# One core, four transformer sub-layers: key weights loaded in two parts, three turns put in another order, and one PSUM bank for each weighted value product

## What is computed

```python
x = x + tanh(g_xattn[0]) * causal_attention(q=layernorm(x), k=ctx, v=ctx)     # 16 heads of 32
x = x + tanh(g_ffn[0]) * ffn_ternary_silu(layernorm(x), w_gate_up, w_proj)    # hidden 2048, weights quantised per 64
x = x + tanh(g_xattn[1]) * cross_attention(layernorm(x), ctx, q_w, k_img_w, v_img_w, o_w, ...)   # 256 keys, rms norm of q and k
x = x + tanh(g_ffn[1]) * bitlinear_ffn(layernorm(x), w_gv, w_out)             # ternary weights, 8-bit activations
```

## Time and profile before

| | |
|---|---|
| median of 3 runs | 1153.73 us (1153.06 to 1154.17) |
| the profiled execution | 1155.84 us, its span (first to last instruction) 1154.0 us |
| TensorE busy | 1112.5 us, 96% of the span |
| VectorE busy | 833.0 us, 72% |
| ScalarE busy | 566.9 us, 49% |
| TensorE's mean granted clock | 0.988 of full |

### The profile page before, as it was taken

One profiled execution on the slowest core, in us unless ns is written; L12 is line 12 of the kernel. 1 busy time (PEld: TensorE's weight loads), 2 busy tenths in 40 slices (PEclk: granted clock), 3 DMA queues, 4 the chain that ended last, 5 costly groups with the idle time before them and its releaser, 6 DMA issues.

```text
span 1154.0 us, 25637 instructions
## 1 busy us (share of the span) xinstructions
PE 1112.5 (96%) x10450; PEld 672.7 (58%) x10450; DVE 833.0 (72%) x1440; ACT 566.9 (49%) x918; POOL 74.2 (6%) x180
## 2 busy tenths in 40 slices
PE   8899999998899999999999999899999999999998
PEld 3455555555677777777777654445454545454543
DVE  5688888777566657566565667687877878777785
ACT  3676666764333333333333442445463737372754
POOL 0000000000000000000001011010101010101010
PEclk9899999999899999999999999999999999999999
DMA  9555555433111010120110201101010100000001
GB/s 371 170 191 175 183 184 174 142 109 111 47 56 41 25 56 19 37 74 19 37 56 19 82 3 37 37 2 56 1 57 1 33 24 17 22 11 11 10 10 37
DMA packets 29124, 79.24 MB, mean 69 GB/s; under 512 B 3025, under 2 KB 3281, under 8 KB 28625
## 3 DMA queue, kind: packets, MB, share of 16 engines
q1 hardware_dynamic: 29008, 77.61, 20.4%
HBM read 65.02 MB, written 12.58 MB: 67 GB/s over the span
## 4 chain that ended last, share of the span: by engine, by line
PE 90%; DVE 5%; ACT 2%; issue 2%; DMA 1%; POOL 0%; ACTq 0%; SPq 0%; DVEq 0%; POOLq 0%
PE bank L537 10%; PE bank L579 10%; PE bank L580 10%; PE bank L662 10%; PE bank L682 9%; PE bank L785 8%; PE bank L773 5%; PE bank L423 5%; PE bank L815 5%; PE bank L735 3%; PE bank L754 3%; PE bank L472 2%; PE bank L493 2%; PE bank L505 2%; PE bank L448 2%
## 5 line engine op out<-in xcount | busy, mean ns | idle before, releaser
L579 PE MATMUL bank<-ARENA,W 128*128 128x256 f16 x1024 | 228.7, 274 | 1.6 <-issue 1.6
L580 PE MATMUL bank<-ARENA,W 128*128 128x256 f16 x1024 | 228.7, 274 | 0.0
L989 ACT ACTIVATE ARENA<-bank 128x512 f32<-128x512 f32 (+3 forms) x143 | 92.9, 689 | 86.3 <-PE bank L423 31.4
L537 PE MATMUL bank<-ARENA 128*128 128x512 f32 x256 | 120.3, 614 | 2.0 <-DMA ARENA<-in_wkv 2.0
L662 PE MATMUL bank<-W,ARENA 128*128 128x512 bf16 x512 | 121.0, 379 | 0.7 <-DVE ARENA L1399 0.7
L785 PE MATMUL bank<-W,ARENA 128*128 128x512 bf16 x512 | 119.6, 383 | 0.7 <-DVE W L1697 0.3
L682 PE MATMUL bank<-ARENA 128*128 128x512 f32 x256 | 116.8, 599 | 0.0
L579 PEld LDWEIGHTS bank<-ARENA,W 128*128 128x128 bf16 x1024 | 100.5, 98 | 20.8 <-issue 2.3
L580 PEld LDWEIGHTS bank<-ARENA,W 128*128 128x128 bf16 x1024 | 100.5, 98 | 18.2
L1557 DVE SCALAR_TENSOR_TENSOR ARENA<-bank,ARENA 128x512 f32<-128x512 f32 x64 | 48.0, 750 | 83.7 <-PE bank L580 78.2
L989 ACT ACTIVATE ARENA<-ARENA 128x512 f16<-128x512 f32 x64 | 40.3, 630 | 130.9 <-DVE ARENA L1557 128.1
(11 more groups left out here) (179 smaller groups left out, 1787.6 us busy)
## 6 DMA issues: line engine op xcount, KB each, us to landing
W<-in_w SPq DMA_DIRECT2D x48, 512.0 KB, 4.1
ARENA<-in_w SPq DMA_DIRECT2D x24, 512.0 KB, 3.6
kv_store<-ARENA SPq DMA_DIRECT2D x32, 256.0 KB, 4.2
W<-kv_store SPq DMA_DIRECT2D x15, 512.0 KB, 3.9
ARENA<-in_ctxT SPq DMA_DIRECT2D x8, 512.0 KB, 3.8
X<-in_x SPq DMA_DIRECT2D x8, 512.0 KB, 6.2
ARENA<-in_ctx SPq DMA_DIRECT2D x8, 512.0 KB, 5.8
out<-X SPq DMA_DIRECT2D x16, 256.0 KB, 2.1
```

Of the source, the lines that this page charges most:

```text
L537: mm = pe.matmul(bank, bufA["KT"][:, b % 2 * KD + k, t * P:(t + 1) * P], W[:, k, :], start=(k == 0), stop=(k == KD - 1 and what == 1))
L579: pe.matmul(bank[:, i * S:(i + 1) * S], W0[:, at:at + P], xt_half(b, 0)[:, k, :], start=(k == 0), stop=False)
L580: mm = pe.matmul(bank[:, i * S:(i + 1) * S], W0[:, at:at + P], xt_half(b, 1)[:, k, :], start=False, stop=(k == KD - 1))
L989: return act.activation(to, src, ACT.Copy)
```

## The change

Five things are edited. (1) The 1 MB of key weights is loaded as two halves of 512 KB with the bias row (`vec`) between them, and `a_project` waits for the second half (`ld_wk2`) ahead of its third input block. (2) In turns 1 and 8 (`late`) VectorE does the second block of scores, `a_max_parts` and `a_max_rows` ahead of `a_ternary(b, 0)`. (3) In turn 8 the first input of stage B is normalised, transposed (into banks 6 and 7) and split earlier, on all engines; the last value projection `a_project(7, 3)` goes to its former place, into bank 1; the largest weight (`m_largest`) is found ahead of `a_max_rows(b, 1)`, and `a_ternary(7, 2)` comes after the whole chain of `m_scl`. (4) At the start of stage B `a_turn_sums(7)` goes to bank 5 and lies between the two parts of `b_gate_up(0, 1)`, and `b_project(0, 0)` comes after `b_gate_up(0, 2)`. (5) In the first turns of stage C each weighted value has a bank of its own, `c_turn_x(1)` moves behind `b_project(7, 6)`, and in the turn of sequence 1 `c_project_q(2, 1)` comes ahead of the output products, and `c_max_rows(1)` ahead of `c_add_out(0, 1)`. Turns 2 to 7 of stage A, stage B after its first three steps, and stage C from turn 3 on are left as they were.

```diff
--- before.py
+++ after.py
-    ld_cst ld_gc ld_x0 ld_x1 ld_kt0 ld_kt1 ld_rv0 ld_rv1 ld_w00 ld_w01 ld_w02 ld_w1a ld_w1b ld_wk ld_wv ld_sel ld_wqo ld_kb ld_row ld_wn
+    ld_cst ld_gc ld_x0 ld_x1 ld_kt0 ld_kt1 ld_rv0 ld_rv1 ld_w00 ld_w01 ld_w02 ld_w1a ld_w1b ld_wk ld_wk2 ld_wv ld_sel ld_wqo ld_kb ld_row ld_wn
...
-        diag = scrA["t"].bitcast(F32)[:, 0:P]
+        diag = scrA["raw0"][:, 0, 0:P]
...
         def bank_of_kv(b, i):
-            return 5 if (b, i) == (0, 1) else (1, 1, 6, 7)[i]
+            return {(0, 1): 5, (NB - 1, 3): 1}.get((b, i), (1, 1, 6, 7)[i])
...
-        places.last = {4: (s.a_pvr, 2 * NB), 5: (s.a_sumr, 2 * NB), 6: (s.b_xy, 2 * NB - 1), 7: (s.b_xy, 2 * NB),
+        places.last = {4: (s.a_pvr, 2 * NB), 5: (s.a_otr, 3 * NB - 2), 6: (s.b_xy, 2 * NB - 1), 7: (s.b_xy, 2 * NB),
...
-        places.turn(1, ("pq0 xt0", "pq1 tq1 w1 w2 w3", "mt kt0 w0", "kt1 tq0 xt1"))
-        for turn in range(2, NB):
+        places.turn(1, ("pq0 kt0 w0 xt0", "pq1 tq1 w1 xt1", "mt tq0 w2", "kt1 w3"))
+        places.turn(2, ("pq0 po0 w0 xt0", "po1 w1 qt1 w3", "pq1 kt0 tq1 w2", "kt1 mt tq0 qt0 xt1"))
+        for turn in range(3, NB):
             places.turn(turn, ("g0 v1 g3 pq0 v6 v7 ut0.0 y0 xt0", "v0 po1 v3 g4 v5 g7 tq1 w1 w2 w3", "po0 g2 kt0 v4 pq1 w0 qt1 ut1.1 y1",
                                "g1 v2 kt1 g5 g6 mt tq0 ut0.1 qt0 ut1.0 xt1"))
...
-            sp.dma_start(bufA["wkv"][:, 0, :], wkv[:, 0:KD * D]).then_inc(s.ld_wk, 16)
+            sp.dma_start(bufA["wkv"][:, 0, 0:2 * D], wkv[:, 0:2 * D]).then_inc(s.ld_wk, 16)
             sp.dma_start(bufA["tmp"][:, 0, :], vec[:, 0:D]).then_inc(s.ld_kb, 16)
+            sp.dma_start(bufA["wkv"][:, 0, 2 * D:KD * D], wkv[:, 2 * D:KD * D]).then_inc(s.ld_wk2, 16)
...
                 if (b, g) == (NB - 1, 2):
-                    pe.wait_ge(s.b_xl, 2)
+                    pe.wait_ge(s.a_kvr, 4 * NB)
...
+                if (b, g) == (NB - 1, 0):
+                    pe.wait_ge(s.b_xl, 2)
                 for j in range(4):
-                    pe.wait_ge(*ringA[4 + j].freed(f"pr{g}", b + 1))
+                    if (b, g, j) != (NB - 1, 0, 3):
+                        pe.wait_ge(*ringA[4 + j].freed(f"pr{g}", b + 1))
...
             def a_turn_sums(turn, b):
-                pe.wait_ge(*ringA[1].freed("ot2", turn))
+                if b < NB - 1:
+                    pe.wait_ge(*ringA[1].freed("ot2", turn))
                 pe.wait_ge(s.a_sumr, 2 * b + 2)
-                turned(banks[1], [scrA["SS"][:, half, t * P:(t + 1) * P] for half in range(2) for t in range(TB)],
+                turned(banks[1 if b < NB - 1 else 5], [scrA["SS"][:, half, t * P:(t + 1) * P] for half in range(2) for t in range(TB)],
                        keep["identf"]).then_inc(s.a_ot, 1)
...
-                    pe.wait_ge(*ringA[at].freed(f"kv{i}", turn))
+                    pe.wait_ge(*ringA[at].freed("kv0" if (b, i) == (NB - 1, 3) else f"kv{i}", turn))
                 for k in range(KD):
+                    if not what and k == 2:
+                        pe.wait_ge(s.ld_wk2, 16)
...
                         to, sem, value = bank_c(f"bx{t}", f)
                         pe.wait_ge(sem, value)
                     else:
-                        to = banks[1 - t]
-                        pe.wait_ge(*(ringA[0].freed("sc2", NB) if t else ringA[1].freed("kv0", NB)))
+                        to = banks[6 + t]
+                        pe.wait_ge(*((s.a_ex, 16 * (NB - 2) + 14) if t else (s.a_kvr, 4 * NB - 1)))
                     pe.wait_ge(s.b_xn, 2 * f + t + 1)
...
                 if q == 1:
                     pe.wait_ge(s.m_scl, 1)
-                    pe.wait_ge(s.a_otr, 3 * NB - 2)
...
                 a_scores(b, 1)
+                if not front:
+                    b_turn_x(0)
                 if end:
                     a_sum(turn, e, 1)
+                if end and front:
                     a_project(turn, b, 3)
                 a_group_sum(turn, b, 1)
...
                 if front:
                     a_project(turn, f, 0)
                 else:
-                    b_turn_x(0)
+                    a_project(turn, b, 3)
                 a_probs(b, 1)
                 a_scores(b, 2)
...
             for b in range(NB):
                 last = b == NB - 1
                 for p in range(8):
-                    if p or b:
-                        b_gate_up(b, p)
                     if (b, p) == (0, 0):
                         b_gate_up(0, 0, (1,), (1,))
                         a_weigh(NB + 1, NB - 1, 1)
                         a_sum(NB + 1, NB - 1, 1)
+                    elif (b, p) == (0, 1):
+                        b_gate_up(0, 1, (0,))
                         a_turn_sums(NB + 1, NB - 1)
-                    if (b, p) == (0, 1):
+                        b_gate_up(0, 1, (1,))
                         a_turn_out(NB + 1, NB - 1)
+                    else:
+                        b_gate_up(b, p)
+                    if (b, p) == (0, 2):
+                        b_project(0, 0)
...
                     elif not last or p < 6:
-                        if p or b:
+                        if p > 1 or b:
                             b_project(*divmod(8 * b + p - 1, 8))
-            c_turn_x(1)
-
             c_scores(0, 0)
             b_project(NB - 1, 6)
+            c_turn_x(1)
             c_scores(0, 1)
             b_project(NB - 1, 7)
             b_sum_squares(NB - 1)
...
             c_scores(1, 0)
             c_project_q(2, 0)
             c_scores(1, 1)
+            c_project_q(2, 1)
+            c_scores(1, 2)
             c_project_out(0, 0)
-            c_scores(1, 2)
             c_turn_k(2)
+            c_scores(1, 3)
             c_project_out(0, 1)
-            c_scores(1, 3)
-            c_project_q(2, 1)
             c_max_turn(1)
             c_probs(1, 0)
             c_turn_q(2)
...
                 if end:
                     a_weighed(e, 1)
+                    if not front:
+                        b_turn_x(0)
                     a_summed(e, 1)
                 if front:
                     a_signs(f, 0)
-                a_projected(b, 3)
+                    a_projected(b, 3)
...
                 if front:
                     a_projected(f, 0)
                 else:
-                    b_turn_x(0)
+                    a_projected(b, 3)
                 a_probs(b, 1)
...
             c_square_q(2, 0)
+            c_square_q(2, 1)
             c_turn_k(2)
-            c_square_q(2, 1)
             c_probs(1, 0)
             c_turn_q(2)
...
+                    sums = banks[5 if b == NB - 1 else 1].rearrange("p (a t j c) -> p a t j c", a=2, t=TB, c=DH)[:, :, t, :, 0:2]
...
+            def m_largest():
+                v.wait_ge(*own.now())
+                v.tensor_reduce(hs[:, 2:3], keep["wmax"], AX_X, ALU.max).then_inc(*own.up())
+                v.wait_ge(*own.now())
+                v.tensor_scalar(hs[:, 2:3], hs[:, 2:3], 1e-8, None, ALU.max).then_inc(*own.up())
+                v.wait_ge(*own.now())
+                v.tensor_scalar(diag, keep["identf"], hs[:, 2:3], None, ALU.mult).then_inc(s.m_in, 1)
+
             for turn in range(NB + 1):
                 f, b, e, last = turn, turn - 1, turn - 2, turn - 3
                 front, back, end = f < NB, b >= 0, e >= 0
+                late = turn in (1, NB)
                 if back:
                     a_scores(b, 0)
+                    if not front:
+                        v.wait_ge(s.a_xt, 2 * NB)
+                        v.wait_ge(s.b_rstd, 1)
+                        for t in range(TB):
+                            normed(0, t, bufB["xn"]).then_inc(s.b_xn, 1)
                     a_distance(b, 0)
-                    a_ternary(b, 0)
+                    if not late:
+                        a_ternary(b, 0)
                     a_scores(b, 1)
                     a_max_parts(b, 0)
+                    if not front:
+                        b_turn_x(0)
+                    if late:
+                        a_max_rows(b, 0)
                 if front:
                     v.wait_ge((s.ld_x0, s.ld_x1)[f % 2], 16 * (f // 2 + 1))
                     stats(f, s.a_ve)
-                else:
...
-                if back:
+                if back and not late:
                     a_max_rows(b, 0)
...
-                else:
-                    v.wait_ge(s.a_xt, 2 * NB)
-                    v.wait_ge(s.b_rstd, 1)
-                    for t in range(TB):
-                        normed(0, t, bufB["xn"]).then_inc(s.b_xn, 1)
...
                 if end:
                     a_reciprocals(e)
+                if late:
+                    a_ternary(b, 0)
                 if last >= 0:
                     a_add_out(last)
                 if back:
                     a_distance(b, 1)
-                    if not front:
-                        b_turn_x(0)
                     a_ternary(b, 1)
                     a_scores(b, 2)
...
                 if back:
                     a_scores(b, 3)
```

(32 more changed lines are left out.)

8 lines of the change are left out of this document (1 added, 7 removed).

## The result

The changed kernel took 1140.55 us (median of 4 runs, 1139.14 to 1142.06) beside 1153.57 us of the kernel before (4 runs); the ratio is 0.9887, its interval 0.9870 to 0.9904. That is 13.0 us faster, where 17.1 us were forecast. Run again beside other kernels it took 1140.13 us beside 1153.93 us, ratio 0.9873 (0.9854 to 0.9892). The profiled execution took 1139.14 us, with a span of 1137.4 us.

A forecast was written before the change was run, and what follows sets the result against it. TensorE was taken as the bound, losing time to idle waits and half clock in three places. Gains of 2.2 + 11.3 + 3.6 = 17.1 us gave 1136.6 us, within 2.5 us at chance 0.70; 1132 to 1142 us at 0.85.

The forecast's parts named there:

- Part 1: Start of the kernel: key halves bring the first projection some 1.3 us earlier, counted as nothing because a store's landing holds.
- Part 2: Turn 1: VectorE's new order moves a_probs(0, 0) from 33.29 to 31.05 us; 2.2 us gained together with the key halves.
- Part 3: Turn 8 and entry to stage B: 13.8 us of waits and low clock, less new waits, gives 11.3 us.
- Three of the new waits: Turn 8 and stage B entry: 0.55 us for last scores at b_gate_up, 0.6 at a_probs(7, 3), 1.0 at a_weigh(7, 1).
- the 0.4 us at `a_probs(7, 0)`: Turn 8: VectorE's two subtractions between the maxima and their copy make a_probs(7, 0) wait about 0.4 us.
- the two long waits: Turn 8: 2.9 us for the largest weight's chain and 2.6 us at a_scores(7, 2) for b_xl; both were to go.
- Part 4: First turns of stage C: separate banks and new orders remove waits, one of 2.2 us remains at c_turn_x(3); 3.6 us gained.
- More than forecast: Turn 0's stores land earlier (2.4 us) or clock stays up after c_turn_x(3) (1.7 us); both give 1132.5 us; chance 0.12.
- Low clock in turn 8: Rival: four short waits keep TensorE at 1.2 GHz in turn 8, losing 3.3 us, 1140 us; chance 0.12.
- Waits that only move: Rival: turn 8's 9 us reappear in stage B's first b_project, time within 2 us of 1153.7 us; chance 0.03.

The follow-up runs named there:

- whole_keys: The changed kernel with the key weights loaded whole again; 1139.73 us, ratio 0.9883 to the kernel before.
- c_only: The kernel before with only stage C's separate banks and changed orders; 1151.02 us, ratio 0.9974.
- t8_only: The kernel before with only the changes to turn 8 and the entry to stage B; 1143.48 us, ratio 0.9908.
- before_store: The kernel before with the first two stores queued ahead of four loads, nothing else; 1155.20 us, ratio 0.9998.
- t1_only: The kernel before with only the key halves and VectorE's new order in turn 1; 1156.18 us, ratio 1.0015.
- no_t1: The changed kernel with whole keys and VectorE's old order in turn 1; 1140.93 us, ratio 0.9884 to the kernel before.
- early_store_whole: The changed kernel with the first two stores queued ahead of four loads and key weights loaded whole; 1140.18 us, ratio 0.9863 to the kernel before.
- after_again: The changed kernel itself, measured again; 1140.13 us, ratio 0.9873 to the kernel before.
- both: The changed kernel with the first two stores ahead of four loads and c_turn_x(3) behind c_weigh(1, 3); 1134.87 us, ratio 0.9830 to the kernel before.
- early_store: The changed kernel with the first two stores queued ahead of four loads; 1137.12 us, ratio 0.9846 to the kernel before.
- set 3: Third set of follow-up kernels, run on one chip: the changed kernel again and three variants of it; the kernel before took 1153.93 us there.

## Why the prediction was right or wrong

The time fell into the range of 1132 to 1142 us, which had a chance of 0.85, and faster was right; it lies outside the 2.5 us around 1136.6 us, which had 0.70. The gain was 4.1 us less than the forecast.

- **Part 1, key halves worth nothing: right**, though by the traces they are worth less than nothing. The first projection starts 0.87 us earlier instead of 1.3 us. That the store is issued 1.5 us earlier than in the earlier trace rows is not their work: in the four traces with whole keys, the old queue order and full clock it is issued at 19.93 to 20.25 us, in the four with halves at 19.80 to 20.82 us. In SyncE's list it stands behind the load of unit 4 of w0, which by the code waits for ScalarE's signs of unit 1. Turn 8 starts at 256.22 us in `whole_keys` and 0.7 to 1.5 us later in the four traces that have halves besides; the times show no difference.
- **Part 2, turn 1 worth 2.2 us: the wait was named rightly, and this term failed.** `a_probs(0, 0)` does stand behind ScalarE's copy, after some 5 us of waiting. But I took both ends of the difference, 33.29 and 31.05 us, from one execution, and that one was not typical: its first projection ran at half clock (5.40 us, where `c_only`, `t8_only` and `before_store` have 3.70 us), while its copy behind the store started at 27.98 us, earlier than in all eight other traces with the old queue order (29.03 to 29.99 us). In those eight, the old order of VectorE arrives at 32.15 to 32.24 us, 1.1 us before the first end, and the new one at 32.20 to 33.11 us, at least 1.15 us behind the second. That TensorE's late start made VectorE late in that execution fits, but no run isolates it. By the start of turn 8, edits 1 and 2 together cost 0.2 to 1.4 us against the old order at full clock. The times bracket that: `t1_only` is 2.1 us slower than the kernel before, the changed kernel 0.8 us faster than `no_t1`. The prediction said that the execution was 2.1 us over the median and assumed the waits to be of the same order in both; that was the step that failed.
- **Part 3, turn 8 and the entry worth 11.3 us: right.** 11.6 us between the traces, 10.6 us by the times of `t8_only`. From turn 8's first scores to the last gate/up product it is 385.3 to 385.6 us in all ten traces with edits 3 and 4, and 396.4 to 397.5 us in the four without. Three of the new waits were forecast as 0.55, 0.6 and 1.0 us and are 0.7, 0.5 and 0.9 us; the 0.4 us at `a_probs(7, 0)` are not there, and `a_group_sum` waits 0.2 us instead. The clock stays at 1.00 through them in every trace with edit 3, so the low clock of before (4.9 us of its cost) went with the two long waits. The Trainium skill (TensorE: Matmul & The Clock Gate, "A second HAM failure mode: psum-queue depth-cycling") says that frequent short idle times between groups of products, from cycling through PSUM banks, let the clock swing to half. The trace does not show that for the four waits of 0.2 to 0.9 us here, with PEclk 1.00 in 257 to 303 us.
- **Part 4, stage C worth 3.6 us: right in sum.** 3.0 us by the times of `c_only`, 4.8 us between the two traces. The wait at `c_turn_x(3)` is 2.79 us, not 2.2 us. The forecast put one wait of 2.2 us in place of 2.2 and 0.6 us and booked 0.15 us, where its own terms give 0.6 us and the measured wait about nothing: that this small term came near is luck. That the clock falls after it holds in some executions only: the 8.4 us from there on have 1.00 in the changed kernel's first trace, `c_only` and `early_store_whole`, and 0.80 to 0.82 in the five others with this wait. Hence the larger gain between the traces: the trace of before pays the low clock there, that of after does not.
- **The sum.** Of the 4.1 us that are missing, part 2 accounts for most: its 2.2 us and the 0.2 to 1.4 us that edits 1 and 2 cost by the start of turn 8, 2.4 to 3.6 us. The rest, 0.5 to 1.7 us, no run assigns; `t8_only` and `c_only` came out 0.7 and 0.6 us under the forecast by their times, which is less than a measurement tells.
- **The rivals.** "More than forecast" is how the two traces look but not the medians. Its condition on the stores, that they land earlier, was met only when they were queued earlier. Low clock in turn 8 is refuted by each trace with edit 3. Waits that only move happened in turn 1, not where I had looked for them: what VectorE's new order and an earlier store each gave was mostly held by the other.

## What to carry to other kernels

Two bounds that end within half a us of each other hide each other's fix: the new order of VectorE and the early stores are worth at most 0.8 us each and some 3 us together by the start of turn 8, and the times of one alone show nothing. Name the second bound before costing the first, and move both together. A difference that starts in one execution's row needs a second execution of the same code: the profile's clock and a product whose duration shows the clock (3.70 or 5.40 us) tell whether it was a typical one. And a store that releases a buffer belongs ahead of bulk loads that nobody needs yet: they delay it twice, as bytes ahead of it in a full queue, and in the issuing engine's list when one of them waits for its buffer.

## What the hardware showed that I had not expected

**The same wait is followed by a low clock in one execution and not in another.** The wait of 2.79 us at `c_turn_x(3)`: the stretch behind it in `after_again`, where the earlier trace rows and the stretch of after shown above have 0.50 and 1.00:

```profile
719.60:728.00 8.40, 8.05 (x66) 4.17 (x67) 6.11 (x7) 3.37 (x5) 0.00 (x0) 0.80 0.31 103
```

In `both` TensorE waits 3.22 us for the third group's scores and goes on at full clock, where `early_store` fell to 0.63 after 3.14 us:

```profile
41.63 0.30 PE L435 MATMUL bank<-ARENA 32*128 32x64 bf16 x16 [3.22 <-DVE ARENA L1382]
```

```profile
41.60:49.00 7.40, 7.19 (x121) 4.55 (x122) 5.54 (x11) 4.13 (x8) 0.00 (x0) 1.00 0.38 117
```

A wait of 1.6 us near the end is in the changed kernel and in `both` alike; the clock of the 8 us from there on is 0.79 in the first and 1.00 in the second:

```profile
1116.05 0.61 PE L425 MATMUL bank<-ARENA 128*128 128x128 bf16 x8 [1.60 <-DVE ARENA L1750]
```

```profile
1116.05:1124.05 8.00, 7.34 (x38) 3.71 (x40) 5.17 (x7) 4.06 (x6) 0.00 (x0) 0.79 0.01 2
```

```profile
1112.28 0.61 PE L425 MATMUL bank<-ARENA 128*128 128x128 bf16 x8 [1.61 <-DVE ARENA L1750]
```

```profile
1112.28:1120.28 8.00, 7.56 (x47) 3.88 (x48) 6.61 (x14) 4.01 (x7) 0.00 (x0) 1.00 0.01 2
```

What decides it is not settled. The mean clock goes with most of the spread between executions of one kernel: beside set 3 the kernel before took 1156.4 to 1157.6 us in its three longest runs with a mean clock of 0.988 to 0.990, and 1152.4 us in its shortest with 0.994. The profiled run of `both` is the only one here at a mean clock of 1.00, with no stretch of 10 us below it. After waits of 0.2 to 0.9 us no trace of a kernel with edit 3 shows a low clock in turn 8.

**Where a store lands goes with the bytes ahead of it, and its issue alone does not tell.** Four loads of 512 KB that stood ahead of the first store stand behind it in `early_store`; at the 395 GB/s of the earlier trace rows they take 5.3 us (an estimate). The store is issued 7.4 us earlier (12.68 in place of 20.11 us), and the copy that it releases starts 5.35 us earlier (23.89 in place of 29.24 us). Its place and its issue moved together, and no run moves one alone. Neither tells all: in the trace of before, with the place of `c_only` and issued 1.3 us later, it released the copy 1.15 us earlier (27.98 in place of 29.13 us), and what made that difference stays open.
